# Windowed-attention kernel on one core: each four heads' output products in one visit instead of two, and a new table of slots and banks

## Chip, cores and metric

The kernel runs on one core of a Trainium2 chip. The metric is the device time of one execution in microseconds, as a median of several runs. Engines are named as the profile names them: PE is the matmul engine (TensorE), PEld its weight loads, DVE the vector engine, ACT the scalar engine, POOL GpSimd, SP the engine whose queue issues the DMAs.

## What is computed

Two attention layers follow each other on 64 samples of 14 x 14 tokens with 192 channels. Each layer normalises in 32 groups, projects to 12 heads of 16, adds two relative-position terms to the scores, takes a softmax over 196 keys, multiplies by v, projects back and adds the input.

```python
attn = jnp.einsum('bqd,bkd->bqk', q * scale, k)
rel_h = jnp.einsum('bhwc,hkc->bhwk', qr, Rh)
rel_w = jnp.einsum('bhwc,wkc->bhwk', qr, Rw)
attn = attn.reshape(B * nh, H, W, H, W) + rel_h[:, :, :, :, None] + rel_w[:, :, :, None, :]
attn = jax.nn.softmax(attn.reshape(B * nh, HW, HW), axis=-1)
out = jnp.einsum('bqk,bkd->bqd', attn, v)
...
x = x + _L0_conv_ref(_gn(x), ...)
x = x + _L1_conv_ref(_gn(x), ...)
```

## The kernel before

One unit is one sample in one layer, so there are 128 units. A software pipeline is written out: each turn of the loop on every engine has 12 slots, and work that a table puts at position `at` of a unit is done in slot `at % 12` of turn `at // 12` after that unit's own. In every slot PE makes two pairs of products for two different units: `ps_max` (L510, scores from which DVE takes the row maxima, L704) and `ps_sc` (L523, transposed scores with the maximum folded in, from which ACT makes `probs` by an exponential, L573). `MAX_AT` and `EXP_AT` say where a unit's first head stands. Behind the two pairs of a slot come the jobs of the table `JOBS` that fall on it (each with its position and its bank of `ps_m`), and then the output products.

The jobs, by name: `xT` transposes the input (L420); `g` sums the group statistics (L426); `qk0`, `qk1`, `v` and `y` are projections from high and low fp16 parts (L403); `rel0` to `rel2` are small products for the relative terms on tiles of 64 x 32 of the array (L464); `mT` transposes the maxima (L469); `ot` and `oT` transpose the attention output (L478, L486). `v` and `y` are 12 matmuls each, `qk0` 12, `qk1` 6.

An output product (L542) of one group takes four heads side by side, each on 32 columns of the array, with 98 keys at a time (`kt` 0 and 1); the second half accumulates on the first in the one bank `ps_o`. The program writes four matmuls for a half. The operands are fp32, and the trace shows two records for each, so a half is x8 and both halves are x16. ACT then copies `ps_o` out (L563).

All engines run their own queue in order. PE's next `ps_max` of a bank waits until DVE has reduced the one two heads earlier; `ps_sc` waits likewise for ACT; a job waits until the last reader of its bank is done (`bank_free`); an output product waits until ACT has made the exponentials of its four heads (`s_p`) and has copied `ps_o` (`s_o`). SP issues all DMAs in one order: `q_dram`/`k_dram` out and back in as `q_st`/`k_st`, the relative rows `q_st<-rel_hl`, the maxima row, the result `yo`, the next input `xa`. `ACT_LATER`, `DVE_LATER`, `POOL_AT` and `SP_AT` place each engine's part of a job in its own queue.

Of the kernel before, what the change touches and what calls it, by code (L numbers as in the profile page):

```python
# [15 lines left out]
SIDE = 14  # L16
TOK = SIDE * SIDE
# [5 lines left out]
HEADS = 12  # L23
# [31 lines left out]
HG = 4  # L55
GROUPS = HEADS // HG
# [3 lines left out]
VB = 6  # L60
# [14 lines left out]
def attention_kernel(nc, x_in, w_all, b_qk, b_rows, rel, onehot, lo_rows, ident_in, gmat_in, out):  # L75
    with ExitStack() as ctx:
# [40 lines left out]
        v_st = [sb(f"v_st{i}", [HT, 2, HEADS, PW]) for i in range(VB)]  # L117
# [14 lines left out]
        xn = pair("xn", [CC, 2, TOK])  # L132
# [10 lines left out]
        probs = [sb(f"probs{i}", [HT, 2, TOK]) for i in range(HEADS)]  # L143
        o_sb = pair("o_sb", [128, GROUPS, TOK])
# [10 lines left out]
        ps_o = psum("ps_o", [128, 512])  # L155
# [15 lines left out]
        s_xT = sem("s_xT")  # L171
# [5 lines left out]
        s_g = sem("s_g")  # L177
# [7 lines left out]
        s_qklo = sem("s_qklo")  # L185
        s_v = sem("s_v")
# [7 lines left out]
        s_rlo = sem("s_rlo")  # L194
# [5 lines left out]
        s_mrow = sem("s_mrow")  # L200
# [3 lines left out]
        s_p = sem("s_p")  # L204
        s_o_ps = sem("s_o_ps")
# [40 lines left out]


        LEAD, TAIL = 2, 6
        MAX_AT, EXP_AT = 30, 47

        PV_AT = {(0, 0): 52, (0, 1): 52, (1, 0): 55, (1, 1): 56, (2, 0): 59, (2, 1): 61}
        O_LATER = 1

        JOBS = [(-10, "xT", 1, (s_xT, 1, 1)),
                (63, "ot", 0, (s_on, 1, 1)),
                (4, "qk0", 2, (s_qklo, 2, 1)),
                (5, "qk1", 1, (s_qklo, 2, 2)),
                (65, "oT", 2, (s_olo, 1, 1)),
                (18, "rel0", 0, (s_rlo, 3, 1)),
                (42, "mT", 1, (s_mrow, 1, 1)),  # L260
                (19, "rel1", 2, (s_rlo, 3, 2)),
                (68, "y", 1, (s_yr, 1, 1)),
                (-4, "g", 2, (s_g, 1, 1)),
                (22, "rel2", 2, (s_rlo, 3, 3)),
                (10, "v", 0, (s_v, 1, 1))]
        ORDER = [name for _, name, _, _ in JOBS]
        AT = {name: at for at, name, _, _ in JOBS}
        BANK = {name: bank for _, name, bank, _ in JOBS}
        READ = {name: read for _, name, _, read in JOBS}

        ACT_LATER = {"qk": 0, "mT": 1, "oT": 0, "xT": 0, "rel": 0, "v": 0, "y": 0}
        DVE_LATER = {"bn": 2, "g": 0, "ot": 0, "oT": 0, "qk": 0, "rel": 0}

        POOL_AT = {"mv": -8, "group": -5, "xn": -5, "xhi": -1, "xlo": 3, "y": 72}
        QK_TILES = ((0, 1), (2,))

        SP_AT = {"m": 44, "rel": 23, "qk_out": 6, "q_in": 9, "k_in": 9, "out": 73, "xa": -22}
# [115 lines left out]
        def _(pe):  # L393
# [14 lines left out]
            def job(name, unit, slot, layer):  # L408
# [57 lines left out]
                elif name == "mT":  # L466
                    pe.wait_ge(s_mx, u.n * HEADS + HEADS)
                    bank_free(pe, unit, name)
                    nc.tensor.transpose(ps[0:2 * HEADS, 0:HT], mx[p2][:, :, :].rearrange("p h q -> p (h q)"),  # L469
                                        ident[0:HT, 0:HT]).then_inc(s_mT_ps, 1)  # L470
                elif name == "ot":

                    pe.wait_ge(s_o, u.n * GROUPS + GROUPS)
                    bank_free(pe, unit, name)
                    for h in range(2):
                        for g in range(GROUPS):
                            at = (h * GROUPS + g) * HG * (HD + 1)
# [20 lines left out]

            def iteration(unit, layer):
                for s in range(HEADS):  # L500
# [51 lines left out]
        def _(act):  # L552
            act.wait_ge(s_setup, 1)

            def iteration(unit, layer):
                for s in range(HEADS):

                    for g in range(GROUPS):
                        u = due(unit, s, PV_AT[g, 1] + O_LATER)
                        if u:  # L560
                            act.wait_ge(s_o_ps, u.n * GROUPS + g + 1)
                            wait(act, s_ot_ps, u.n - 1)
                            nc.scalar.copy(o_sb[u.r % 2][:, g, :].rearrange("p (k r b) -> p k r b", r=2, b=SIDE),  # L563
                                           ps_o[:, 0:TOK].rearrange("p (k b r) -> p k r b", r=2, b=SIDE))\
                              .then_inc(s_o, 1)
                    head = head_at(EXP_AT, s)
                    u = due(unit, s, EXP_AT + head)
# [331 lines left out]
```

## Time and profile before

| what | value |
|---|---|
| median of 3 runs | 1927.35 us (1926.01 to 1927.59) |
| the profiled execution | 1927.02 us, span 1925.2 us |
| granted PE clock | 0.996 of full |
| PE busy | 1857.8 us (96%), 34176 matmul records |
| DVE, ACT, POOL busy | 1435.6, 1364.9, 713.3 us |

The first matmul starts at 37.7 us, behind loads and constants. From about 130 us to 1860 us every unit takes the same time. A busy PE is no proof of full use, since a matmul record reaches beyond the moment at which the next one starts. The start of one record to the start of the next is what an instruction costs PE; that is what the prediction reads.

### The profile page before, as it was taken

To read this page: it belongs to the slowest core of one execution; us is meant where nothing else is said; L and a number is where in the kernel's file an instruction comes from. 1 tells how busy PE (TensorE), PEld (TensorE's weight loads), DVE (VectorE), ACT (ScalarE), POOL (GpSimd) and SP (SyncE) were. 2 spreads that over 40 slices of the span, in tenths; PEclk is the share of its full clock that TensorE was granted. 3 is DMA by queue.
4 is the path that set the end of the run, shared out by engine and by line. 5 is a ranking of instruction groups with operands and counts; after the bars stand their busy time and mean duration, and the time that the engine had idled before them with its cause. 6 is when DMAs were issued, how large, how long until landed. Compare 5 with 4: busy or idle time off the path is not lost.

```text
span 1925.2 us, 84394 instructions
## 1 busy us (share of the span) xinstructions
PE 1857.8 (96%) x34176; PEld 1511.5 (79%) x34176; DVE 1435.6 (75%) x3568; ACT 1364.9 (71%) x3201; POOL 713.3 (37%) x1796
## 2 busy tenths in 40 slices
PE   0799999999999999999999999999999999999997
PEld 0678888888888888888888888888888888888885
DVE  6477777777777777777777777777777777777774
ACT  0277777777777777777777777777777777777776
POOL 1333433433434334334334334343343343343331
PEclk9999999999999999999999999999999999999999
DMA  1444444444434444444444444444444444444440
GB/s 39 99 101 102 113 104 108 107 104 108 112 101 113 108 102 110 107 102 112 104 107 108 103 108 112 101 113 105 104 111 107 102 111 105 102 113 104 111 102 25
DMA packets 142171, 197.76 MB, mean 103 GB/s; under 512 B 26455, under 2 KB 109656, under 8 KB 141786
## 3 DMA queue, kind: packets, MB, share of 16 engines
q1 hardware_dynamic: 141786, 192.36, 40.3%
q8 instruction: 274, 4.49, 1.0%
q14 instruction: 111, 0.91, 0.2%
HBM read 97.74 MB, written 57.80 MB: 81 GB/s over the span
## 4 chain that ended last, share of the span: by engine, by line
PE 93%; issue 3%; DVE 2%; POOL 1%; ACT 0%; DMA 0%; POOLq 0%; SPq 0%; ACTq 0%
PE ps_m L403 24%; PE ps_max L510 17%; PE ps_o L542 17%; PE ps_sc L523 13%; PE ps_m L464 11%; PE ps_m L478 4%; PE ps_m L420 2%; PE ps_m L486 2%; PE ps_m L469 1%; PE ps_m L426 1%; DVE k_st L657 0%; POOL yo L840 0%; DVE v_st L650 0%; POOL xn L817 0%; DMA w_raw<-in_b_rows 0%
## 5 line engine op out<-in xcount | busy, mean ns | idle before, releaser
L704 DVE TENSOR_REDUCE mx<-ps_max 98x2 f32<-98x392 f32 x1536 | 834.2, 557 | 237.0 <-PE ps_max L510 222.9
L573 ACT ACTIVATE probs<-ps_sc 98x392 f32<-98x392 f32 x1536 | 735.4, 497 | 171.0 <-PE ps_sc L523 126.0
L510 PE MATMUL ps_max<-k_st,q_st 124*98 124x196 f16 x3072 | 537.8, 257 | 0.6 <-DVE mx L704 0.3
L523 PE MATMUL ps_sc<-q_st,k_st 125*98 125x196 f16 x3072 | 511.3, 247 | 0.6 <-ACT probs L573 0.5
L510 PEld LDWEIGHTS ps_max<-k_st,q_st 124*98 124x98 f16 x3072 | 299.5, 124 | 200.3 <-issue 157.6
L542 PE MATMUL ps_o<-probs,v_st 98*32 98x196 f32 x6144 | 388.7, 340 | 1.9 <-issue 1.1
L523 PEld LDWEIGHTS ps_sc<-q_st,k_st 125*98 125x98 f16 x3072 | 320.5, 124 | 3.5 <-ACT probs L573 1.8
L755 DVE TENSOR_TENSOR rel_hl<-ps_m,rel_hi 128x504 f16<-128x504 f32 (+1 forms) x384 | 216.0, 562 | 85.6 <-ACT rel_hi L618 85.6
L618 ACT ACTIVATE rel_hi<-ps_m,is_lo 128x504 f16<-128x504 f32 (+1 forms) x384 | 225.8, 588 | 31.5 <-PE ps_m L464 31.3
L788 POOL TENSOR_TENSOR msq<-mv 96x2 f32<-96x2 f32 x128 | 24.6, 192 | 586.4 <-DVE mv L730 586.4
L464 PE MATMUL ps_m<-q_st,rel_st 64*32 64x36 f16 (+1 forms) x14336 | 238.0, 209 | 0.3 <-DVE gsm L770 0.3
L464 PEld LDWEIGHTS ps_m<-q_st,rel_st 64*32 64x32 f16 x14336 | 191.5, 101 | 52.3 <-issue 1.3
L798 POOL TENSOR_TENSOR msq<-gsm 96x2 f32<-96x2 f32 x128 | 24.6, 192 | 505.5 <-DVE gsm L770 505.5
L403 PE MATMUL ps_m<-xn_hi,w_hi 98*128 98x196 f16 (+1 forms) x768 | 193.1, 251 | 8.3 <-POOL xn_lo L830 8.3
L542 PEld LDWEIGHTS ps_o<-probs,v_st 98*32 98x32 f32 x6144 | 134.2, 108 | 77.2 <-issue 22.9
L403 PE MATMUL ps_m<-xn_lo,w_hi 96*128 96x196 f16 x768 | 192.1, 250 | 0.0
L403 PE MATMUL ps_m<-xn_hi,w_lo 96*128 96x196 f16 x768 | 191.4, 249 | 0.0
L716 DVE TENSOR_TENSOR qk_hl<-ps_m,qk_hl 128x392 f16<-128x392 f32 (+1 forms) x256 | 117.0, 457 | 79.0 <-ACT qk_hl L585 79.0
L563 ACT COPY o_sb<-ps_o 128x196 f32<-128x196 f32 x384 | 123.9, 323 | 59.0 <-PE ps_o L542 46.7
L585 ACT CAST qk_hl<-ps_m 128x392 f16<-128x392 f32 (+1 forms) x256 | 103.5, 404 | 84.0 <-PE ps_m L403 82.4
L840 POOL TENSOR_TENSOR yo<-yr,xa 98x384 f32<-98x384 f32 x128 | 128.7, 1005 | 55.4 <-ACT yr L632 55.4
L403 PE MATMUL ps_m<-w_hi,xn_hi 98*98 98x192 f16 (+1 forms) x512 | 132.5, 259 | 0.0
(74 smaller groups left out, 2963.8 us busy)
## 6 DMA issues: line engine op xcount, KB each, us to landing
q_st<-q_dram SPq DMA_DIRECT2D x128, 294.0 KB, 3.9
k_st<-k_dram SPq DMA_DIRECT2D x256, 147.0 KB, 3.9
q_dram<-qk_hl SPq DMA_DIRECT2D x128, 147.0 KB, 2.7
k_dram<-qk_hl SPq DMA_DIRECT2D x128, 147.0 KB, 2.8
q_st<-rel_hl SPq DMA_DIRECT2D x256, 73.5 KB
q_st<-rel_hl SPq DMA_DIRECT2D x256, 64.3 KB
xa<-in_x SPq DMA_DIRECT2D x64, 147.0 KB
x<-yo SPq DMA_DIRECT2D x64, 147.0 KB
```

What stands on the lines that cost most here:

```text
L403: last = nc.tensor.matmul(dst, weights(a, c, k), moving(b, c, k), start=n == 0, stop=n == len(terms) - 1)
L464: last = nc.tensor.matmul(to, rel_st[:, lay, axis, w:w + RW], q, start=True, stop=True)
L510: last = nc.tensor.matmul(ps_max[head % 2][0:HT, h * TOK:h * TOK + TOK], q_st[u.n % QB][0:R_MAX, head, h, :], k_st[u.n % QB][0:R_MAX, head ...
L523: last = nc.tensor.matmul(ps_sc[head % 2][0:HT, kt * TOK:kt * TOK + TOK], k_st[u.n % QB][0:STACK, head, kt * HT:kt * HT + HT], q_st[u.n % ...
L542: last = nc.tensor.matmul(ps_o[32 * j:32 * j + 32, 0:TOK], v_st[u.n % VB][:, kt, head_of(head), :], p[:, kt, :], start=kt == 0, stop=kt == 1)
L563: nc.scalar.copy(o_sb[u.r % 2][:, g, :].rearrange("p (k r b) -> p k r b", r=2, b=SIDE), ps_o[:, 0:TOK].rearrange("p (k b r) -> p k r b", r ...
L573: nc.scalar.activation(probs[head][:, :, :], ps_sc[head % 2][0:HT, 0:2 * TOK].rearrange("p (k t) -> p k t", k=2), ACT.Exp, scale=1.0 / (QS ...
L618: nc.scalar.activation(rel_part(rel_hi[u.r % 2], n), rel_bank(n), ACT.Identity, scale=is_lo[:, 0:1]).then_inc(s_rhi, 1)
L704: nc.vector.reduce_max(mx[u.r % 2][:, head, :], ps_max[head % 2][0:HT, 0:2 * TOK].rearrange("p (q k) -> p q k", q=2), axis=AX.X).then_inc( ...
L716: nc.vector.tensor_tensor(qk_hl[u.r % 2][:, 1, at, :], ps_m[BANK[f"qk{j}"]][:, 0:len(tiles) * TOK].rearrange("p (c t) -> p c t", t=TOK), q ...
L755: nc.vector.tensor_tensor(rel_part(rel_hl[u.r % 2], n), rel_bank(n), rel_part(rel_hi[u.r % 2], n), ALU.subtract).then_inc(s_rlo, 1)
L840: nc.gpsimd.tensor_tensor(yo[p2][:, :, :], yr[p2][:, :, :], xa[u.n % XB][:, :, :], ALU.add)\
```

## The change

The two halves of the keys stand in one visit for every group of four heads, and the wait on the four exponentials and on `ps_o` stands ahead of it. The table `PV_AT` has three places in place of six, two of which were one slot before (52). All other tables are new: positions, three banks, and the places in the queues of ACT, DVE, POOL and SP. No instruction of computation is added or removed.

```diff
-        MAX_AT, EXP_AT = 30, 47
-        PV_AT = {(0, 0): 52, (0, 1): 52, (1, 0): 55, (1, 1): 56, (2, 0): 59, (2, 1): 61}
+        MAX_AT, EXP_AT = 29, 45
+        PV = ((0,), (1,), (2,))
+        PV_AT = (50, 53, 56)
         O_LATER = 1
...
-                (-4, "g", 2, (s_g, 1, 1)),
-                (22, "rel2", 2, (s_rlo, 3, 3)),
-                (10, "v", 0, (s_v, 1, 1))]
+                (-5, "g", 0, (s_g, 1, 1)),
+                (20, "rel2", 2, (s_rlo, 3, 3)),
+                (9, "v", 2, (s_v, 1, 1)),
+                (59, "ot", 0, (s_on, 1, 1))]
...
-        SP_AT = {"m": 44, "rel": 23, "qk_out": 6, "q_in": 9, "k_in": 9, "out": 73, "xa": -22}
+        SP_AT = {"m": 41, "rel": 19, "qk_out": 3, "q_in": 9, "k_in": 9, "out": 72, "xa": -21}
...
-                    for (g, kt), at in PV_AT.items():
-                        u = due(unit, s, at)
+                    for i, groups in enumerate(PV):
+                        u = due(unit, s, PV_AT[i])
                         if u:
-                            n = u.n * GROUPS + g
-                            if kt == 0:
+                            if i == 0:
                                 wait(pe, s_v, u.n + 1)
-                                wait(pe, s_p, u.n * HEADS + HG * g + HG)
-                                wait(pe, s_o, n)
-                            for j in range(HG):
-                                head = HG * g + j
-                                p = probs[head]
-                                last = nc.tensor.matmul(ps_o[32 * j:32 * j + 32, 0:TOK],
-                                                        v_st[u.n % VB][:, kt, head_of(head), :], p[:, kt, :],
-                                                        start=kt == 0, stop=kt == 1)
-                            if kt == 1:
+                            wait(pe, s_p, u.n * HEADS + HG * groups[-1] + HG)
+                            wait(pe, s_o, u.n * len(PV) + i)
+                            for n, g in enumerate(groups):
+                                for kt in range(2):
+                                    for j in range(HG):
+                                        head = HG * g + j
+                                        last = nc.tensor.matmul(ps_o[32 * j:32 * j + 32, n * TOK:n * TOK + TOK],
+                                                                v_st[u.n % VB][:, kt, head_of(head), :],
+                                                                probs[head][:, kt, :], start=kt == 0, stop=kt == 1)
                                 last.then_inc(s_o_ps, 1)
```

On PE, this is what stands before around the third group's output products (heads 8 to 11): the first head's scores of the next unit, the first half, two slots without a job, the second half.

```order
L523 MATMUL ps_sc<-q_st,k_st 98x196 [waits s_p,s_m0]
L523 MATMUL ps_sc<-q_st,k_st 98x196
L542 MATMUL ps_o<-probs,v_st 32x196 [waits s_o,s_p,s_v]
L542 MATMUL ps_o<-probs,v_st 32x196 x3
L510 MATMUL ps_max<-k_st,q_st 98x196 [waits s_mx]
L510 MATMUL ps_max<-k_st,q_st 98x196
L523 MATMUL ps_sc<-q_st,k_st 98x196 [waits s_p]
L523 MATMUL ps_sc<-q_st,k_st 98x196
L510 MATMUL ps_max<-k_st,q_st 98x196 [waits s_mx]
L510 MATMUL ps_max<-k_st,q_st 98x196
L523 MATMUL ps_sc<-q_st,k_st 98x196 [waits s_p]
L523 MATMUL ps_sc<-q_st,k_st 98x196
```

The second half (L542 x4) is the next row there. Now, on PE at the same place of the program (line numbers are one higher), the scores ahead are those of head 11 itself, then `rel2`, then both halves:

```order
L524 MATMUL ps_sc<-q_st,k_st 98x196 [waits s_p]
L524 MATMUL ps_sc<-q_st,k_st 98x196
L465 MATMUL ps_m<-q_st,rel_st 32x84 [waits s_rlo]
L465 MATMUL ps_m<-q_st,rel_st 32x84
L465 MATMUL ps_m<-q_st,rel_st 32x6x2 x2
L465 MATMUL ps_m<-q_st,rel_st 32x84 x2
L465 MATMUL ps_m<-q_st,rel_st 32x6x2 x26
L543 MATMUL ps_o<-probs,v_st 32x196 [waits s_o,s_p]
L543 MATMUL ps_o<-probs,v_st 32x196 x7
L511 MATMUL ps_max<-k_st,q_st 98x196 [waits s_mx]
L511 MATMUL ps_max<-k_st,q_st 98x196
```

So the third group's visit moved from one slot after its last head's scores to the same slot, with only `rel2` between, and `rel2` now waits for the low part of `rel1` (`s_rlo`), whose bank it takes, where it waited for `g` before.

In SP's queue, the loads of `q_st` and `k_st` stood ahead of the four DMAs of the relative rows before:

```order
L345 DMA q_st<-mrow 1x24x98 [waits s_mrow]
L365 DMA q_st<-q_dram 64x1x2352 [waits s_qd0]
L371 DMA k_st<-k_dram 32x1x2352 [waits s_kd0]
L371 DMA k_st<-k_dram 32x1x2352
L354 DMA q_st<-rel_hl 32x1176 [waits s_rlo]
L354 DMA q_st<-rel_hl 32x1176
L354 DMA q_st<-rel_hl 28x1176 x2
```

Now they stand behind them:

```order
L346 DMA q_st<-mrow 1x24x98 [waits s_mrow]
L355 DMA q_st<-rel_hl 32x1176 [waits s_rlo]
L355 DMA q_st<-rel_hl 32x1176
L355 DMA q_st<-rel_hl 28x1176 x2
L366 DMA q_st<-q_dram 64x1x2352 [waits s_qd3]
L372 DMA k_st<-k_dram 32x1x2352 [waits s_kd3]
L372 DMA k_st<-k_dram 32x1x2352
```

The load of `q_st` is thus held back until DVE has made the low part of `rel2` of an earlier unit.

## Rows read from the trace of the kernel before

**Rows 1.** Windows: one unit's time; columns are named in the first line.
```profile
core 0: us, PE busy (x) PEld busy (x) DVE busy (x) ACT busy (x) POOL busy (x), PEclk, DMA share, GB/s
1000.00:1014.33 14.33, 14.33 (x270) 11.69 (x269) 10.97 (x28) 10.64 (x26) 5.57 (x16) 1.00 0.43 108
```

**Rows 2.** Timeline of PE, one unit: start, duration, line, tiles, count.
```profile
1002.00 0.25 PE L403 MATMUL ps_m<-xn_hi,w_hi 98*128 98x196 f16 x1
...
1002.93 0.25 PE L403 MATMUL ps_m<-xn_hi,w_lo 96*128 96x196 f16 x1
1003.11 0.87 PE L542 MATMUL ps_o<-probs,v_st 98*32 98x196 f32 x16
1003.91 0.37 PE L510 MATMUL ps_max<-k_st,q_st 124*98 124x196 f16 x2
1004.12 0.33 PE L523 MATMUL ps_sc<-q_st,k_st 125*98 125x196 f16 x2
...
1006.70 0.66 PE L464 MATMUL ps_m<-q_st,rel_st 64*32 64x84 f16 x40
1007.29 0.54 PE L542 MATMUL ps_o<-probs,v_st 98*32 98x196 f32 x8
1007.76 0.37 PE L510 MATMUL ps_max<-k_st,q_st 124*98 124x196 f16 x2
1007.96 0.33 PE L523 MATMUL ps_sc<-q_st,k_st 125*98 125x196 f16 x2
1008.14 0.25 PE L403 MATMUL ps_m<-w_hi,oT_hi 98*98 98x192 f16 x1
...
1009.13 0.26 PE L426 MATMUL ps_m<-mv,gmat 96*96 96x4 f32 x2
1009.32 0.54 PE L542 MATMUL ps_o<-probs,v_st 98*32 98x196 f32 x8
1009.79 0.37 PE L510 MATMUL ps_max<-k_st,q_st 124*98 124x196 f16 x2
1010.00 0.33 PE L523 MATMUL ps_sc<-q_st,k_st 125*98 125x196 f16 x2
...
1010.60 0.52 PE L464 MATMUL ps_m<-q_st,rel_st 64*32 64x84 f16 x32
1011.05 0.28 PE L403 MATMUL ps_m<-w_hi,xn_hi 98*98 98x192 f16 x1
...
1012.08 0.33 PE L510 MATMUL ps_max<-k_st,q_st 124*98 124x196 f16 x2
1012.25 0.33 PE L523 MATMUL ps_sc<-q_st,k_st 125*98 125x196 f16 x2
1012.52 0.54 PE L542 MATMUL ps_o<-probs,v_st 98*32 98x196 f32 x8
1012.99 0.37 PE L510 MATMUL ps_max<-k_st,q_st 124*98 124x196 f16 x2
...
1016.32 0.25 PE L403 MATMUL ps_m<-xn_hi,w_hi 98*128 98x196 f16 x1
```

**Rows 3.** Timeline of ACT and PE: two steady exponentials, and the last output products.
```profile
1010.37 0.89 ACT L573 ACTIVATE probs<-ps_sc 98x392 f32<-98x392 f32 x2
...
1912.68 0.89 ACT L573 ACTIVATE probs<-ps_sc 98x392 f32<-98x392 f32 x2
...
1913.66 0.87 PE L542 MATMUL ps_o<-probs,v_st 98*32 98x196 f32 x16 [0.85 <-ACT probs L573]
```

**Rows 4.** Timeline of DVE and POOL: from the group sums to the normalised input.
```profile
1009.43 0.16 DVE L770 COPY gsm<-ps_m 96x4 f32<-96x4 f32 x1
...
1012.88 0.51 POOL L825 CAST xn_hi<-xn 96x392 f16<-96x392 f32 x1
...
1014.31 0.93 POOL L830 TENSOR_TENSOR xn_lo<-xn,xn_hi 96x392 f16<-96x392 f32 x1
```

**Rows 5.** SP's issues in order of time, then q_st's load's time to landing.
```profile
1011.97 2.88 SPq L354 DMA_DIRECT2D q_st<-rel_hl  x4
...
DMA to landing us min/median/max: 3.5/3.9/4.5
```

More of the change, by code:

```diff
@@ L248, in attention_kernel @@
         LEAD, TAIL = 2, 6
-        MAX_AT, EXP_AT = 30, 47
-        PV_AT = {(0, 0): 52, (0, 1): 52, (1, 0): 55, (1, 1): 56, (2, 0): 59, (2, 1): 61}
+        MAX_AT, EXP_AT = 29, 45
+        PV = ((0,), (1,), (2,))
+        PV_AT = (50, 53, 56)
         O_LATER = 1
[L254 to L262, printed above, removed]
-                (-4, "g", 2, (s_g, 1, 1)),
-                (22, "rel2", 2, (s_rlo, 3, 3)),
-                (10, "v", 0, (s_v, 1, 1))]
+        JOBS = [(-11, "xT", 1, (s_xT, 1, 1)),
+                (2, "qk0", 2, (s_qklo, 2, 1)),
+                (4, "qk1", 1, (s_qklo, 2, 2)),
+                (64, "oT", 2, (s_olo, 1, 1)),
+                (17, "rel0", 0, (s_rlo, 3, 1)),
+                (41, "mT", 1, (s_mrow, 1, 1)),
+                (18, "rel1", 2, (s_rlo, 3, 2)),
+                (67, "y", 1, (s_yr, 1, 1)),
+                (-5, "g", 0, (s_g, 1, 1)),
+                (20, "rel2", 2, (s_rlo, 3, 3)),
+                (9, "v", 2, (s_v, 1, 1)),
+                (59, "ot", 0, (s_on, 1, 1))]
         ORDER = [name for _, name, _, _ in JOBS]
@@ L269, in attention_kernel @@
         READ = {name: read for _, name, _, read in JOBS}
-        ACT_LATER = {"qk": 0, "mT": 1, "oT": 0, "xT": 0, "rel": 0, "v": 0, "y": 0}
-        DVE_LATER = {"bn": 2, "g": 0, "ot": 0, "oT": 0, "qk": 0, "rel": 0}
-        POOL_AT = {"mv": -8, "group": -5, "xn": -5, "xhi": -1, "xlo": 3, "y": 72}
+        ACT_LATER = {"qk": 0, "mT": 0, "oT": 0, "xT": 0, "rel": 0, "v": 0, "y": 1}
+        DVE_LATER = {"bn": 0, "g": 0, "ot": 1, "oT": 0, "qk": 0, "rel": 0}
+        POOL_AT = {"mv": -7, "group": -5, "xn": -3, "xhi": 0, "xlo": 0, "y": 77}
         QK_TILES = ((0, 1), (2,))
-        SP_AT = {"m": 44, "rel": 23, "qk_out": 6, "q_in": 9, "k_in": 9, "out": 73, "xa": -22}
+        SP_AT = {"m": 41, "rel": 19, "qk_out": 3, "q_in": 9, "k_in": 9, "out": 72, "xa": -21}
         def head_at(base, slot):
@@ L471, in job @@
                 elif name == "ot":
-                    pe.wait_ge(s_o, u.n * GROUPS + GROUPS)
+                    pe.wait_ge(s_o, u.n * len(PV) + len(PV))
                     bank_free(pe, unit, name)
@@ L556, in iteration @@
                 for s in range(HEADS):
-                    for g in range(GROUPS):
-                        u = due(unit, s, PV_AT[g, 1] + O_LATER)
+                    for i, groups in enumerate(PV):
+                        u = due(unit, s, PV_AT[i] + O_LATER)
                         if u:
-                            act.wait_ge(s_o_ps, u.n * GROUPS + g + 1)
+                            act.wait_ge(s_o_ps, u.n * GROUPS + groups[-1] + 1)
                             wait(act, s_ot_ps, u.n - 1)
-                            nc.scalar.copy(o_sb[u.r % 2][:, g, :].rearrange("p (k r b) -> p k r b", r=2, b=SIDE),
-                                           ps_o[:, 0:TOK].rearrange("p (k b r) -> p k r b", r=2, b=SIDE))\
+                            nc.scalar.copy(o_sb[u.r % 2][:, groups[0]:groups[-1] + 1, :]
+                                           .rearrange("p g (k r b) -> p (g k) r b", r=2, b=SIDE),
+                                           ps_o[:, 0:len(groups) * TOK].rearrange("p (k b r) -> p k r b", r=2, b=SIDE))\
                               .then_inc(s_o, 1)
```

## Prediction

> **What bounds the kernel now.** I read the table of windows first: in a stretch as long as one unit PE is busy for all of its 14.33 us, while DVE works 10.97 us and ACT 10.64 us [rows 1]. A full PE bar proves little, so I then read PE's timeline by starts. The reader is to see that each start follows the last at the same small distance: the two pairs of a slot are 0.17 us apart, 0.085 us a matmul (12.08 to 12.25), and nowhere in the unit does a matmul wait for another engine. The first matmul of `qk0` at 1002.00 comes again at 1016.32, 14.33 us later by the windows' length [rows 1, 2]. So PE's own instructions, with what it loses when it changes from one kind of tile to another, are the time: 128 x 14.33 = 1834 us of the 1925 us span, and the rest is the start and the drain. What PE saves per unit counts in full, until some wait becomes visible.
>
> **What the change removes.** It removes no matmul, only boundaries. Their price, by starts [rows 2]:
> - Into an output visit from full-width work: the pair of scores at 12.25 is followed at 12.52, 0.27 us and not 0.17; for `qk0`, 2.93 to 3.11 is 0.18 and not 0.085. So 0.09 us more (I take 0.09).
> - The visit itself up to the next `ps_max`: 0.47 us for one half (12.52 to 12.99, also at 7.29 and 9.32), and 0.80 us for both (3.11 to 3.91). Two halves apart are 0.94, together 0.80.
> - Out of it: the pair behind it takes 0.21 or 0.20 us (3.91 to 4.12, 7.76 to 7.96) and not 0.17, so 0.04 more.
>
> One half on its own therefore costs 0.09 + 0.47 + 0.04 = 0.60 us, both together 0.93 us. The four lone halves now:
> - third group, two visits behind scores: 0.60 + 0.60;
> - second group, first half, behind `rel1`: no entry to take off, since `rel1` is itself tiled, 0.47 + 0.04 = 0.51;
> - second group, second half, behind `g`: 0.51. The way from `g` to it is 0.19 us (9.13 to 9.32), and the way from `g` to an ordinary pair is in no row. It can be no less than two steps of 0.03 to 0.085 and no more than the 0.19. I take 0.13, near the middle, so 0.06 us goes here, with 0 and 0.10 as ends.
>
> Sum removed: 0.60 + 0.60 + 0.51 + 0.51 + 0.06 = 2.28 us a unit.
>
> **What it adds.** The second group's visit now follows `mT`, a full-width job: 0.93 us. The third follows `rel2`; `rel2` to the next thing is 0.45 us (10.60 to 11.05), and I take that exit as it is, so 0.84 us. `rel1` is now followed by an ordinary pair, which takes 0.04 more, as a pair behind a visit does; bounds are 0 and 0.09 (an entry's price). `v` no longer follows `rel2`: it took 1.03 us (11.05 to 12.08) where `y`, the same 12 matmuls, takes 0.99 (8.14 to 9.13), so 0.04 less. Sum added: 0.93 + 0.84 + 0.04 - 0.04 = 1.77 us. PE's own work per unit goes down by 2.28 - 1.77 = **0.51 us**, to 13.82 us, if nothing waits. That is 65 us over 128 units.
>
> The Trainium skill (TensorEngine Tiling (Array Packing), Tiling Modes, Key Properties) says that a change of tiling mode drains the array. By that rule every visit pays one way in and one way out whatever stands beside it, so two visits less would bring 2 x (0.60 + 0.60 - 0.93) = 0.54 us, 69 us in all. The trace agrees for full-width neighbours, but from `rel1` into a visit [rows 2] no extra shows beyond what `rel2` pays to any successor, and I keep the 0.51 of the rows.
>
> **The wait that it adds.** The third group's visit needs the exponential of head 11, and that head's scores are now made in the same slot. Count from the slot's start. The scores start at 0.17; ACT starts their exponential 0.37 us after them (10.00 to 10.37), at 0.54, if it is free, and it is, since the slot before gave it only one more exponential after `rel1`. It runs 0.50 us (two in 0.89, the second starting 0.39 after the first), until 1.04 [rows 2, 3]. PE takes up an output visit 0.10 us after that: at the end of the run two exponentials end at 1912.68 + 0.89 = 1913.57 and the visit that waited for them starts at 1913.66 or 1913.67 [rows 3]. So it can start at 1.14. PE itself arrives at 0.17 + 0.26 (scores and entry into `rel2`, as into a visit) + 0.45 = 0.88. It **waits 0.26 us**; after an idle gap the first of the four passes is a little shorter, and I take 0.24 us (bounds 0.20 and 0.28). Behind the waiting matmul stand all later pairs, so DVE and ACT get theirs later too. No job is there to cover it. Before, the same exponential had most of a slot more. Over about 125 units in which the slot is full: 30 us.
>
> **Other waits that come nearer.** I walked the slots in the new order with these prices. Slots 5, 6 and 7 last 2.0, 1.1 and 1.5 us, slot 8 lasts 1.7, slot 2 lasts 2.3.
> - `qk0` needs the low part of the normalised input. From `gsm` (9.43) to the end of `xn_hi` (13.39) are 3.96 us, and `xn_lo`, now directly behind it, takes 0.07 to begin and 0.93: 4.96 us [rows 4]. `gsm` starts 0.30 us after `g` (9.13 to 9.43), and now up to 0.70, since a maximum is in front. With 0.05 to react, `qk0` can start 5.3 to 5.7 us after `g`. PE's way from `g` to `qk0` was 7.19 us (9.13 to 16.32); less 2.28 - 0.51 for visits gone in that stretch, less one slot's two pairs 0.34, plus the third visit's 0.80, it is 5.88, and 6.12 with the wait. Just hidden, by 0.2 to 0.8 us.
> - The load of `q_st` now waits in SP's queue for `rel2`. From the start of slot 8: `rel2` ends at 0.9, ACT and DVE make its two parts by about 1.9, the four DMAs take SP 2.88, the load lands 3.9 later (at most 4.5): 8.7 to 9.3 us [rows 5]. `rel0` needs it at 13.82 - (2.0 + 1.1 + 1.5) + 0.43 = 9.65, 9.9 with the wait. Hidden by 0.6 to 1.2 us.
> - DVE's share rises to 10.97 of about 14.06 us, which leaves room; its queue is longest in slots 0 to 2 (division, statistics, two maxima), where my walk finds its maximum due within 0.1 us of PE's need.
>
> **Sum.** 1927.0 (the profiled execution, 0.3 below the median) - 65 + 30 = **1892 us**. The unit's time should be 13.82 + 0.24 = 14.06 us. The ends of the unknown prices are 0.05 us a unit for the exits, 0.04 for the wait, and some 3 us for start and drain, whose latency chains move: 1884 to 1900 for this case.
>
> **Rivals.**
> 1. *No wait shows* (the exponential comes earlier than I count, or `rel2` takes longer). Then 1927 - 65 = 1862 us. Against it stand three durations of rows that leave 0.26 us. Chance 8%.
> 2. *More than one wait shows*: one of the three slim covers fails by 0.1 to 0.25 us a unit, 12 to 31 us more, 1904 to 1923. For it: the covers are estimates of 0.1 to 0.6 us. Chance 14%.
> 3. *No change that can be told* (within 0.2%, 3.9 us): the waits together eat the 0.51. The covers would have to fail by 0.27 us beyond the wait. Chance 3%.
> 4. *Slower, by the load of `q_st`*. It is behind the relative rows and behind their wait for DVE. If it lands more than 0.6 to 1.2 us later than now, PE waits at `rel0` every unit; 0.27 us beyond that the kernel is as slow as before, and at 1 us more beyond, it takes 1927 + 0.73 x 125 = 2018 us or less, as the chain slackens. For it: all relative rows are in front of it in the queue. Against: the four DMAs need 2.88 us only to be issued, so most of their bytes have gone, and landing times spread only from 3.5 to 4.5 [rows 5]. Chance 4%.
>
> **How the numbers follow.** The forecast has 71%. Faster by over 0.2% holds in it and in rivals 1 and 2: 93%. The range reaches from 1880, somewhat below the forecast's own 1884, up to 1910 into rival 2; below lies rival 1 (8%), above the rest of rival 2 and rivals 3 and 4 (some 12%).
>
> **What would show it.** In the new profile the output visits are x16 alone, three a unit, each 0.80 us to the next `ps_max`; the unit repeats every 14.06 us; PE has one wait a unit, on the exponential of ACT ahead of the visit behind `rel2`, with starts 0.7 and not 0.45 us after `rel2` begins. If the gap there is missing, rival 1 is at work. If gaps stand ahead of `qk0`, `rel0` or a `ps_max`, it is rival 2 or 4. I would be wrong above all if a wait that I count as hidden by 0.2 us is not.

## The result and the profile after

| kernel | median | of |
|---|---|---|
| before | 1927.30 us (1926.01 to 1927.59) | 4 runs |
| after | 1894.20 us (1894.12 to 1894.75) | 4 runs |

The ratio is 0.983, with a 95% interval of 0.9813 to 0.9847: 33 us less. The forecast was 1892 us.

The head of the page of the changed kernel:

```profile
span 1892.3 us, 84394 instructions
...
PE 1807.1 (95%) x34176; PEld 1533.1 (81%) x34176; DVE 1401.2 (74%) x3568; ACT 1352.2 (71%) x3201; POOL 712.6 (38%) x1796
```

The window of one unit, with the columns of [rows 1]:

```profile
1000.00:1014.05 14.05, 13.91 (x271) 11.74 (x266) 10.57 (x28) 10.50 (x25) 5.57 (x14) 1.00 0.45 106
```

The number of PE records is the same, 34176, and PE's bar is still nearly full. Unlike before it has a gap in a unit, though: 13.91 us busy of 14.05. PE's timeline, which answers to [rows 2], tells where:

```profile
1003.26 0.26 PE L470 MATMUL ps_m<-ident,mx 98*24 98x98 f32 x1
1003.45 0.87 PE L543 MATMUL ps_o<-probs,v_st 98*32 98x196 f32 x16
1004.25 0.37 PE L511 MATMUL ps_max<-k_st,q_st 124*98 124x196 f16 x2
...
1004.72 0.67 PE L465 MATMUL ps_m<-q_st,rel_st 64*32 64x84 f16 x40
1005.31 0.37 PE L511 MATMUL ps_max<-k_st,q_st 124*98 124x196 f16 x2
...
1006.69 0.26 PE L427 MATMUL ps_m<-mv,gmat 96*96 96x4 f32 x2
1006.80 0.35 PE L511 MATMUL ps_max<-k_st,q_st 124*98 124x196 f16 x2
1006.99 0.33 PE L524 MATMUL ps_sc<-q_st,k_st 125*98 125x196 f16 x2
1007.25 0.52 PE L465 MATMUL ps_m<-q_st,rel_st 64*32 64x84 f16 x32
1007.91 0.87 PE L543 MATMUL ps_o<-probs,v_st 98*32 98x196 f32 x16
1008.72 0.37 PE L511 MATMUL ps_max<-k_st,q_st 124*98 124x196 f16 x2
1009.00 0.37 PE L524 MATMUL ps_sc<-q_st,k_st 125*98 125x196 f16 x2
```

Every visit is x16 and is followed 0.80 or 0.81 us later by the next `ps_max` (1003.45 to 1004.25, 1007.91 to 1008.72). From `rel2` to the visit behind it are 0.66 us (1007.25 to 1007.91), where `rel2` to its successor took 0.45 us in [rows 2]. The records overlap, so of these 0.21 us more PE's row shows only 0.14 us as idle (14.05 - 13.91); the distance of starts gives the whole. The weight loader's line in the list of waits names its cause (engine line waited for: us in total, times, longest):

```profile
PEld ps_o L543 <- ACT probs L574: 32.0, 128, 0.8
...
PE ps_sc L524 <- DMA q_st<-mrow: 2.7, 6, 0.9
```

The first is the forecast wait, 128 times, 0.25 us each: idle time of the weight loader, of which 0.21 us reach the matmuls. The second was not forecast. It shows in the timeline too: behind the pair at 1008.72 the next one starts 0.28 us later, not 0.21. ACT's timeline shows the releaser of the first:

```profile
1007.36 0.50 ACT L574 ACTIVATE probs<-ps_sc 98x392 f32<-98x392 f32 x1 [0.78 <-PE ps_sc L524]
```

The scores of head 11 start at 1006.99, their exponential at 1007.36, and it ends at 1007.86. The visit starts at 1007.91.

From here on "the unit" is the mean over 105 units in the middle of the run, worked out from the starts of `xT` of unit 15 and unit 120: 14.339 us before ((1745.99 - 240.43) / 14.339 = 105) and 14.084 us after ((1716.22 - 237.38) / 105). A unit in which nothing is late takes 14.05 us. 128 x (14.339 - 14.084) = 33 us, the whole difference of the medians. In the experiments this product and the difference of the medians agree within 5 us, but for one run (7 us), whose unit holds stretches at a lower clock, as said there.

### The profile page after: what moved, and what is told of

Same layout as the page of the kernel before. It is cut to its first block, busy times and chain, and to the rows that moved or that the text cites. A ratio compares the mean times of both kernels' runs of the same rounds, so it can differ in the third digit from the quotient of the medians.

```text
span 1892.3 us, 84394 instructions
## 1 busy us (share of the span) xinstructions
PE 1807.1 (95%) x34176; PEld 1533.1 (81%) x34176; DVE 1401.2 (74%) x3568; ACT 1352.2 (71%) x3201; POOL 712.6 (38%) x1796
## 4 chain that ended last, share of the span: by engine, by line
PE 86%; issue 4%; ACT 4%; DVE 2%; DMA 2%; SPq 1%; POOL 1%; POOLq 0%; ACTq 0%
PE ps_m L404 23%; PE ps_max L511 17%; PE ps_o L543 16%; PE ps_sc L524 13%; PE ps_m L465 8%; PE ps_m L479 4%; ACT probs L574 3%; PE ps_m L421 2%; PE ps_m L487 2%; DMA q_st<-mrow 1%; PE ps_m L470 1%; SPq L337 1%; PE ps_m L427 1%; DVE k_st L658 0%; POOL yo L841 0%
## 5 line engine op out<-in xcount | busy, mean ns | idle before, releaser
L574 ACT ACTIVATE probs<-ps_sc 98x392 f32<-98x392 f32 x1536 | 722.9, 497 | 201.8 <-PE ps_sc L524 157.7
L511 PEld LDWEIGHTS ps_max<-k_st,q_st 124*98 124x98 f16 x3072 | 292.1, 124 | 133.0 <-issue 80.3
L543 PE MATMUL ps_o<-probs,v_st 98*32 98x196 f32 x6144 | 335.7, 336 | 18.8 <-ACT probs L574 1.8
L543 PEld LDWEIGHTS ps_o<-probs,v_st 98*32 98x32 f32 x6144 | 159.9, 109 | 93.6 <-ACT probs L574 32.0
L404 PE MATMUL ps_m<-w_hi,xn_hi 98*98 98x192 f16 (+1 forms) x512 | 127.7, 249 | 1.8 <-DVE rel_hl L756 1.7
```

The lines of the kernel that those rows point to most:

```text
L404: last = nc.tensor.matmul(dst, weights(a, c, k), moving(b, c, k), start=n == 0, stop=n == len(terms) - 1)
L511: last = nc.tensor.matmul(ps_max[head % 2][0:HT, h * TOK:h * TOK + TOK], q_st[u.n % QB][0:R_MAX, head, h, :], k_st[u.n % QB][0:R_MAX, head ...
L543: last = nc.tensor.matmul(ps_o[32 * j:32 * j + 32, n * TOK:n * TOK + TOK], v_st[u.n % VB][:, kt, head_of(head), :], probs[head][:, kt, :], ...
L574: nc.scalar.activation(probs[head][:, :, :], ps_sc[head % 2][0:HT, 0:2 * TOK].rearrange("p (k t) -> p k t", k=2), ACT.Exp, scale=1.0 / (QS ...
```

## Experiments

Ratios are to the kernel before on the same chip (1926.97 to 1927.29 us there), with the 95% interval. "Old table" is the kernel before with the named edit, "new table" the changed one.

### What one visit in place of two is worth

**Old table, third group at 60, second at 55.** It changes three numbers of the kernel before and leaves its banks and queues alone.
```diff
-        PV_AT = {(0, 0): 52, (0, 1): 52, (1, 0): 55, (1, 1): 56, (2, 0): 59, (2, 1): 61}
+        PV_AT = {(0, 0): 52, (0, 1): 52, (1, 0): 55, (1, 1): 55, (2, 0): 60, (2, 1): 60}
```


> The old table again, all three groups merged, but groups 1 and 2 put at positions 55 and 60: behind rel1, so that g stays late enough, and in slot 0, between the empty slots, so that no maximum pair comes under 1.0 us after the one two slots earlier. Boundaries: 0.51 + 0.06 + 0.60 - 2 x 0.33 = 0.50 us a unit less, a unit of 13.84 us. Theory: no wait appears, 1864 us, which is 30 us faster than the changed kernel with only three numbers of the old table touched. Rival: a new table was needed for the merge, and waits for ACT, DVE or POOL (qk0's cover by POOL is down to about 0.1 us) eat 0.25 us and more: 1895 us or above.

Measured: 1866.85 us, ratio 0.9687 (0.9673 to 0.9701), unit 13.847 us. Its window of one unit:
```profile
1000.00:1013.84 13.84, 13.84 (x269) 11.82 (x268) 10.87 (x28) 10.55 (x26) 5.57 (x14) 1.00 0.42 111
```
And one line of PE's timeline that comes again 13.84 us later:
```profile
1011.90 0.50 PE L420 MATMUL ps_m<-ident,xa 98*96 98x98 f32 x4
...
1025.74 0.50 PE L420 MATMUL ps_m<-ident,xa 98*96 98x98 f32 x4
```
PE waits for nothing in the unit, and the boundaries alone took 14.339 - 13.847 = 0.49 us off it. The new table is not needed for the gain. It is 27 us slower than this edit.

**New table with the first two groups split again** (halves at 50 and 51, 53 and 54, the third group whole at 56):
```diff
-        PV_AT = (50, 53, 56)
+        PV_AT = (51, 54, 56)
+        HALF_AT = {(0, 0): 50, (0, 1): 51, (1, 0): 53, (1, 1): 54, (2, 0): 56, (2, 1): 56}
...
```
The loop of the output products goes over `HALF_AT` here, one half at a time, with the waits ahead of the first half.

> The changed kernel's table, but groups 0 and 1 are split again into two visits (positions 50 and 51, 53 and 54); group 2 stays merged behind rel2. If the gain comes from the merge, at my prices group 0 costs 0.27 us more and group 1 0.47 + 0.04 - 0.04 - 0.33 = 0.14 us more a unit, together 0.40: 1941 us, slower than before. Rival: the gain of the change comes from its new positions and banks, and the split costs little: 1894 to 1905 us.

Measured: 1944.33 us, 1.0089 (1.0074 to 1.0104), unit 14.476. Splitting the two groups costs 14.476 - 14.084 = 0.39 us a unit, where 0.40 was expected. This kernel has four lone halves, as many as the kernel before, and with its new wait it takes 0.14 us a unit more than that. So the gain of the change is the merging, and none of it the layout.

**Old table, 56 and 61**: the merged visits stand where the second halves stood.
```diff
-        PV_AT = {(0, 0): 52, (0, 1): 52, (1, 0): 55, (1, 1): 56, (2, 0): 59, (2, 1): 61}
+        PV_AT = {(0, 0): 52, (0, 1): 52, (1, 0): 56, (1, 1): 56, (2, 0): 61, (2, 1): 61}
```


> The old table with one thing changed: the first halves of groups 1 and 2 are moved to where their second halves stood (positions 56 and 61), so that all three visits hold both halves. By boundaries alone PE saves 0.51 + 0.60 - 2 x 0.33 - 0.04 = 0.40 us a unit, and the time would be 1876 us (rival: only PE's own instructions count, any merge pays). My theory says that two waits appear: g comes 0.47 us earlier and waits about 0.3 us for DVE's low part of rel1, whose bank it takes; and slots 11, 0 and 1 stand three in a row with nothing but their two pairs (0.34 us each), where the maximum pair of a slot must come at least about 1.0 us after the one two slots earlier (0.37 to the reduction, 0.56 for it, 0.05 to react), so that slot 1 waits about 0.34 us for DVE. Then the unit takes about 14.5 us and the time is 1940 to 1960 us, slower than before.

Measured: 1973.27 us, 1.0241 (1.0224 to 1.0258), unit 14.710. The sign was as expected, the size was not. PE's timeline:
```profile
1003.33 0.25 PE L403 MATMUL ps_m<-w_hi,oT_lo 96*98 96x192 f16 x1
1003.75 0.30 PE L426 MATMUL ps_m<-mv,gmat 96*96 96x4 f32 x2 [0.18 <-DVE rel_hl L755]
...
1007.43 0.33 PE L510 MATMUL ps_max<-k_st,q_st 124*98 124x196 f16 x2
1007.60 0.33 PE L523 MATMUL ps_sc<-q_st,k_st 125*98 125x196 f16 x2
1008.07 0.37 PE L510 MATMUL ps_max<-k_st,q_st 124*98 124x196 f16 x2
```
Two waits stand there, each in nearly every unit. `g` starts 0.42 us behind the last matmul of `y` in place of 0.08, since DVE hasn't finished `rel1`'s low part, which `g` waits for to have its bank: the half visit behind `rel1` had covered that. And the maximum pair at 1008.07 starts 0.47 us behind the pair at 1007.60 in place of 0.17. The two waits, 0.34 and 0.31 us, leave 14.339 + 0.65 - 14.710 = 0.28 us for what the boundaries saved, where 0.40 was expected: that is most of why it is slower than the 1940 to 1960 us.

**Old table, third group at 59** with the second at 55:
```diff
-        PV_AT = {(0, 0): 52, (0, 1): 52, (1, 0): 55, (1, 1): 56, (2, 0): 59, (2, 1): 61}
+        PV_AT = {(0, 0): 52, (0, 1): 52, (1, 0): 55, (1, 1): 55, (2, 0): 59, (2, 1): 59}
```


> The merged old table once more (55 and 60 gave a unit of 13.85 us without a wait), but group 2 at 59, in slot 11, so that slots 0 and 1 hold only their two pairs (0.38 and 0.34 us) and slot 2 starts 0.72 us after slot 0. Boundaries are the same. Theory: a maximum pair must come about 1.04 us after the one two slots earlier (0.41 to the reduction behind a visit, 0.56, 0.05, and a start of the weights 0.04 late costs nothing), so slot 2 waits 0.3 us for DVE: 14.16 us a unit, 1905 us. Rival: the place of the visit among short slots does not matter, 1867 us.

Measured: 1907.87 us, 0.9899 (0.9883 to 0.9916), unit 14.186, as expected. It isolates the second of those waits. PE's timeline:
```profile
1003.72 0.37 PE L510 MATMUL ps_max<-k_st,q_st 124*98 124x196 f16 x2
...
1004.10 0.33 PE L510 MATMUL ps_max<-k_st,q_st 124*98 124x196 f16 x2
1004.27 0.33 PE L523 MATMUL ps_sc<-q_st,k_st 125*98 125x196 f16 x2
1004.75 0.37 PE L510 MATMUL ps_max<-k_st,q_st 124*98 124x196 f16 x2
```
and DVE's:
```profile
1004.13 2.27 DVE L704 TENSOR_REDUCE mx<-ps_max 98x2 f32<-98x392 f32 x4 [0.71 <-PE ps_max L510]
```
The maxima alternate between two banks. DVE starts on the pair of 1003.72 at 1004.13 and needs 2.27 / 4 = 0.57 us, so the same bank is free at 1004.70, and PE refills it at 1004.75, 1.03 us after it was filled last. Without the wait it would come after 0.38 + 0.34 = 0.72 us. A slot with nothing in it but its two pairs therefore can't stand beside another such slot without a wait of 0.3 us. The half visit at 59 or 61 was the filling.

### The new wait behind rel2

**New table, third group one slot later.**
```diff
-        PV_AT = (50, 53, 56)
+        PV_AT = (50, 53, 57)
```


> The changed kernel with the visit of group 2 one slot later (57, behind v). In the changed kernel 0.306 us lie between the last product of rel2 and that visit, against 0.098 from rel2 to v before. Theory: 0.208 us of it is the wait for the exponential of head 11, and it goes; the entry from full-width work (0.09) and the pair behind rel2 (0.04) come in its place, so PE saves 0.08 us a unit. But the scores of head 0 of the next unit, which stand in slot 9, now come 1.0 us earlier, and the DMA of the maxima row lands only about 1.0 us ahead of them at the median: a new wait of about 0.25 us on average, 1905 to 1925 us. Rival: the 0.306 us are the cost of changing from one tiling to another, no wait: then the gap stays in some form, and nothing else waits, 1894 us or more by 5.

Measured: 1979.64 us, 1.0272 (1.0255 to 1.0289), unit 14.807. The wait on the exponential is gone, but PE waits elsewhere, and longer:
```profile
1007.75 0.52 PE L465 MATMUL ps_m<-q_st,rel_st 64*32 64x84 f16 x32
1008.20 0.37 PE L511 MATMUL ps_max<-k_st,q_st 124*98 124x196 f16 x2
1008.49 0.37 PE L524 MATMUL ps_sc<-q_st,k_st 125*98 125x196 f16 x2
1009.24 0.26 PE L404 MATMUL ps_m<-w_hi,xn_hi 98*98 98x192 f16 x1 [0.39 <-DVE rel_hl L756]
```
and in its list of waits:
```profile
PE ps_sc L524 <- DMA q_st<-mrow: 27.4, 37, 1.8
```
`rel2` to its successor is 0.45 us again, so what stood behind it in the changed kernel was a wait of 0.66 - 0.45 = 0.21 us. But `v` is given `rel2`'s bank, and now has only one slot's pairs between them: it starts 0.75 us after the scores, not 0.17 (0.83 us in most units, where the scores themselves are in time). The visit had covered the two readers of that bank, ACT and DVE. The expectation had left this out, and so was wrong by more than 50 us. (New banks in the change have `g` and `v` only, two jobs and not three.) The maxima row, too, is late in 37 units and not in 6.

The execution that was profiled took 1990.67 us, 11 us more than the median, and its clock tells why. Where the wait for the maxima row was long, PE's granted clock could fall behind it from full to half, 2.4 to 1.2 GHz, for 6.8 us (a row of PE, then the window behind it with the columns of [rows 1]):
```profile
1141.98 0.37 PE L524 MATMUL ps_sc<-q_st,k_st 125*98 125x196 f16 x2 [1.30 <-DMA q_st<-mrow]
```
```profile
1142.60:1149.40 6.80, 6.80 (x49) 5.65 (x47) 1.97 (x5) 2.58 (x6) 2.12 (x5) 0.50 0.51 126
```
There are five such stretches between 200 us and the drain, each begun in or within 0.6 us behind a wait of PE on this DMA of 1.1 to 1.8 us; three waits of 1.2 to 1.4 us were followed by none. A unit with one takes 3.9 to 4.4 us more, the wait included. The unit of 14.807 us is a mean with three of them in it. The median unit is 14.65 us, as in the next run.

**The same, with the next input's load behind the maxima row in SP's queue.**
```diff
-        PV_AT = (50, 53, 56)
+        PV_AT = (50, 53, 57)
...
-        SP_AT = {"m": 41, "rel": 19, "qk_out": 3, "q_in": 9, "k_in": 9, "out": 72, "xa": -21}
+        SP_AT = {"m": 41, "rel": 19, "qk_out": 3, "q_in": 9, "k_in": 9, "out": 72, "xa": -19}
```


> As the run with the visit of group 2 at 57, and SP issues xa behind the maxima row (-19 for -21), which gives that DMA about 0.5 us back. Theory: most of the new wait goes, 0.05 us a unit stays, about 1888 us. If the two runs are equal, the wait at head 0's scores is not that DMA.

Measured: 1962.27 us, 1.0183 (1.0168 to 1.0198), unit 14.653. The 17 us between the medians of the two runs went with the maxima row's DMA: its waits, and the stretches at half clock behind them. How they divide is not shown; the mean clock was 0.990 to 0.994 in the four other executions there and 0.995 to 0.997 here. The rest of the loss is `v`'s bank. 1888 us was expected, so this was a miss of the same cause.

**The same again, with `v` and `rel2` in different banks.**
```diff
-        JOBS = [(-11, "xT", 1, (s_xT, 1, 1)),
+        JOBS = [(-11, "xT", 0, (s_xT, 1, 1)),
...
-                (9, "v", 2, (s_v, 1, 1)),
+                (9, "v", 0, (s_v, 1, 1)),
...
-                (59, "ot", 0, (s_on, 1, 1))]
+                (59, "ot", 1, (s_on, 1, 1))]
```


> The changed kernel with group 2 at 57 and xa at -19 as in the earlier run, and v in bank 0, ot in bank 1, xT in bank 0. In the earlier run v, which takes rel2's bank, waited 0.66 us for DVE's low part of rel2, because the visit that had covered it was gone from between. Theory: with another bank for v that wait goes, no wait for an exponential is left, and the unit takes 14.05 - 0.21 + 0.09 + 0.04 = 13.97 us, with 0.02 for late DMAs of the maxima row 13.99: 1881 us. Rival: the head-0 scores then find that DMA late in most units, as I had expected of the first of these runs: 1895 us or more.

Measured: 1879.46 us, 0.9754 (0.974 to 0.9769), unit 13.990. The place behind `rel2` was good for the boundary and bad for the exponential: leaving it saves 0.21 us and costs an entry and a pair's 0.04, 0.13 us by [rows 2], so that 0.08 us should remain. The unit fell by 0.06 us against the kernel with the same SP queue and the visit at 56 (14.054, below).

**A longer `rel2`**: `RELB`, the blocks of relative products of the three jobs, from (6, 6, 2) to (6, 2, 6), so that `rel2` covers the exponential, with `v` and `ot` in other banks and four DMAs of SP's queue at other places.
```diff
-RELB = (6, 6, 2)
+RELB = (6, 2, 6)
...
-                (9, "v", 2, (s_v, 1, 1)),
+                (9, "v", 0, (s_v, 1, 1)),
...
-                (59, "ot", 0, (s_on, 1, 1))]
+                (59, "ot", 2, (s_on, 1, 1))]
...
-        SP_AT = {"m": 41, "rel": 19, "qk_out": 3, "q_in": 9, "k_in": 9, "out": 72, "xa": -21}
+        SP_AT = {"m": 41, "rel": 20, "qk_out": 3, "q_in": 7, "k_in": 7, "out": 72, "xa": -19}
```


> The changed kernel with the relative rows cut 6, 2, 6 and not 6, 6, 2: the short piece stands in slot 6 and a long one (0.60 and not 0.45 us) between head 11's scores and the visit of group 2. PE's own work is the same. So that nothing else waits, v takes bank 0 and ot bank 2, SP issues the loads of q_st and k_st at position 7, the relative rows at 20 behind them, and xa at -19. Theory: the wait for head 11's exponential goes from 0.21 to 0.06 us a unit and the waits for the maxima row go: 14.09 - 0.15 - 0.03 = 13.91 us a unit, 1872 us. Rival (the gap ahead of the visit is the price of a change of tiling, not a wait): 1890 us.

Measured: 1941.92 us, 1.0074 (1.0059 to 1.0089), unit 14.493. A miss, again by a bank:
```profile
1006.18 0.33 PE L524 MATMUL ps_sc<-q_st,k_st 125*98 125x196 f16 x2
1006.94 0.24 PE L404 MATMUL ps_m<-xn_hi,w_hi 98*128 98x196 f16 x1 [0.42 <-DVE on L742]
```
`qk0` starts 0.76 us after the scores, not 0.17: it has the bank that `ot` got, and DVE reads `ot` for the division until then.

**The same with `ot` in bank 1 and `xT` in bank 0.**
```diff
-        JOBS = [(-11, "xT", 1, (s_xT, 1, 1)),
+        JOBS = [(-11, "xT", 0, (s_xT, 1, 1)),
...
-                (59, "ot", 2, (s_on, 1, 1))]
+                (59, "ot", 1, (s_on, 1, 1))]
```


> The long-rel2 kernel again (rows cut 6, 2, 6, v in bank 0, loads of q_st at 7, relative rows at 20, xa at -19), with ot in bank 1 and xT in bank 0, so that qk0 no longer takes the bank that DVE's division of ot still reads. In its predecessor the gap ahead of the visit behind rel2 fell to 0.191 us (rel1, as long, pays 0.128 to any successor), and qk0 waited 0.58 us for that bank. Theory: with the bank changed the 0.58 us go and nothing comes: a unit of 14.49 - 0.58 = 13.91 us, 1871 us. Rival: qk0 was late for another reason (the low part of the normalised input from POOL, whose cover I put at 0.1 to 0.3 us): then part of the wait stays, 1885 us or more.

Measured: 1870.3 us, 0.9703 (0.9689 to 0.9718), unit 13.910, as expected. PE:
```profile
1007.66 0.66 PE L465 MATMUL ps_m<-q_st,rel_st 64*32 64x84 f16 x40
1008.32 0.87 PE L543 MATMUL ps_o<-probs,v_st 98*32 98x196 f32 x16
```
The visit now follows a `rel2` of x40 by 0.66 us, where `rel1` of the same size is followed by 0.59. Most of the wait is filled with work that has to be done anyway: 14.054 - 13.910 = 0.14 us a unit.

### The maxima row's DMA

**Changed kernel, the input's load behind the maxima row and not ahead of it in SP's queue.**
```diff
-        SP_AT = {"m": 41, "rel": 19, "qk_out": 3, "q_in": 9, "k_in": 9, "out": 72, "xa": -21}
+        SP_AT = {"m": 41, "rel": 19, "qk_out": 3, "q_in": 9, "k_in": 9, "out": 72, "xa": -19}
```


> The changed kernel with one number changed: SP issues the next input (xa) at position -19 and not -21, so that the small DMA of the maxima row is issued ahead of it, about 0.5 us earlier. In the changed kernel's trace the scores of head 0 wait in 11 of 112 units for that DMA, up to 0.6 us, 0.03 us a unit on average. Theory: these waits go, 1890 us, and every unit takes 14.05 us. Rival: these waits come from something else that is there in some units (a busy DMA engine of the q_st load): no change, 1894 us.

Measured: 1890.24 us, 0.9809 (0.9795 to 0.9824), unit 14.054. In the list of waits PE and its weight loader have no line on `mrow` any more. (The 11 units of the expectation count the same units twice: in the middle of the run 6 weight loads and 5 matmuls waited.) 14.084 - 14.054 = 0.03 us a unit is what the late rows cost, 4 us in all. The interval overlaps that of the change (0.9813 to 0.9847), so that the 4 us rest on the unit and on the waits gone, not on the medians alone.

### How far it goes

**Old table, the first group directly behind `rel0` at 54** (from 52), `mT` one slot later, and ACT's part of `mT` in its own slot:
```diff
-        PV_AT = {(0, 0): 52, (0, 1): 52, (1, 0): 55, (1, 1): 56, (2, 0): 59, (2, 1): 61}
+        PV_AT = {(0, 0): 54, (0, 1): 54, (1, 0): 55, (1, 1): 55, (2, 0): 60, (2, 1): 60}
...
-                (42, "mT", 1, (s_mrow, 1, 1)),
+                (43, "mT", 1, (s_mrow, 1, 1)),
...
-        ACT_LATER = {"qk": 0, "mT": 1, "oT": 0, "xT": 0, "rel": 0, "v": 0, "y": 0}
+        ACT_LATER = {"qk": 0, "mT": 0, "oT": 0, "xT": 0, "rel": 0, "v": 0, "y": 0}
```


> The merged old table (55 and 60), and group 0 moved from 52, behind qk0, to 54, directly behind rel0, with mT one position later (43, and ACT's part of it without delay), so that it stands ahead of rel1. By boundaries: qk0 gives up its exit into a visit (0.18 to 0.08), rel0's exit of 0.13 goes into the visit and not into mT, mT's exit goes into rel1 (0.19 and not 0.09 plus 0.18 of the scores before it): 0.09 us a unit less, a unit of 13.76 us, 1855 us, if no wait comes. Rival: what a visit costs does not depend on what stands ahead of it (a drain is paid for every change of tiling, rel1 into a visit too): 1867 us. A wait by g for rel1's low part or by the visit for exponentials would show as a gap and make it slower than 1867.

Measured: 1928.28 us, 1.0007 (0.9997 to 1.0017), unit 14.339. PE's timeline:
```profile
1001.75 0.25 PE L403 MATMUL ps_m<-xn_hi,w_lo 96*128 96x196 f16 x1
1002.42 0.51 PE L486 MATMUL ps_m<-ident,on 98*96 98x98 f32 x4 [0.42 <-DVE qk_hl L716]
```
and its list of waits:
```profile
PE ps_m L486 <- DVE qk_hl L716: 51.2, 123, 0.4
```
1855 us was expected, so this was a miss. The boundary was saved as priced, and all of it and more was lost at one place: `oT`, which takes `qk0`'s bank, starts 0.67 us after the last matmul of `qk1` and not 0.08, since DVE still reads `qk0`. The visit at 52 had stood between them.

**The same, with one tile in `qk0` and two in `qk1`**:
```diff
-        QK_TILES = ((0, 1), (2,))
+        QK_TILES = ((0,), (1, 2))
```


> The last kernel (visits at 54, 55 and 60) with qk0 taking one tile (6 matmuls) and qk1 two (12), where it was two and one. In the last run every boundary came out as priced, 13.76 us a unit without waits, but oT, which takes qk0's bank, waited 0.58 us for DVE's low part of qk0: the visit of group 0 had stood between them and covered it. Now 12 matmuls of qk1 stand between, 0.51 us more, and qk0's read is shorter by a tile. Theory: the 0.58 us go, nothing else waits, 13.76 us a unit and 1855 us, the fastest. Rival: the saving behind tiled work is paid again elsewhere, because DVE and POOL are near their limit of slots (qk1 now ends later than mT or rel1 need): 1867 us or more.

Measured: 1853.27 us, 0.9619 (0.9602 to 0.9636), unit 13.747: the fastest kernel of this study, 3.8% faster than before and 2.2% faster than the change. Its window of one unit:
```profile
1000.00:1013.75 13.75, 13.75 (x274) 11.85 (x267) 10.77 (x27) 10.63 (x25) 5.56 (x15) 1.00 0.44 112
```
And in PE's timeline the two visits that stand behind tiled work:
```profile
1005.16 0.67 PE L464 MATMUL ps_m<-q_st,rel_st 64*32 64x84 f16 x40
1005.76 0.87 PE L542 MATMUL ps_o<-probs,v_st 98*32 98x196 f32 x16
...
1007.12 0.67 PE L464 MATMUL ps_m<-q_st,rel_st 64*32 64x84 f16 x40
1007.71 0.87 PE L542 MATMUL ps_o<-probs,v_st 98*32 98x196 f32 x16
```
`qk0` is now half as much to read, and 12 matmuls stand between it and `oT` in place of 6, which covers the reading again. From `rel` to the visit are 0.60 and 0.59 us, the same as from `rel` to an ordinary pair (0.59). The entry into the visit costs nothing there.

## Why the prediction held

**PE was the bound, and what its instructions save counts in full.** Right. The two kernels without a recurring wait have the unit that prices by starts gave ahead of the runs, 13.84 and 13.76 us: it is 13.847 us, and 13.747 with one entry into a visit less (0.09 of the 0.10). And 128 times the difference of the units is the difference of the medians for the change, and is within 3 us of it for these two.

**The removed and added boundaries, 0.51 us.** Right within 0.02. The old table with its visits merged saved 0.49 us without a wait. In the changed kernel, 14.084 less the two waits, 0.21 and 0.03, is 13.85 us, 0.49 below before. Both halves cost 0.80 us to the next pair, as in [rows 2]. The price that no row had, from `g` to a pair, was taken as 0.13 us; it is 0.11 (1006.69 to 1006.80), and the pair behind it takes 0.19 in place of 0.17, which makes up the 0.13. The Trainium skill's rule (TensorEngine Tiling (Array Packing), Tiling Modes, Key Properties), by which each change of mode drains the array, gave 0.54 us. Here the trace agrees for full-width neighbours, where a visit pays 0.09 us going in and 0.04 behind it. Behind `rel` it does not: the kernels with a visit there show nothing beyond `rel`'s own exit, and so the lone half behind `rel1` in the kernel before had no entry to give back.

**The new wait.** The right place, the right releaser, in every unit. Its size was 0.21 us and not 0.24 (0.26 by the durations). The term that was mis-sized is the time to react, taken as 0.10 us from the end of the run [rows 3]. Here the exponential ends at 1007.86 and the visit starts at 1007.91, 0.05 us. With 0.05 in place of 0.10 the durations give 0.21. The further 0.02 us that the prediction took off, for a shorter first pass after an idle gap, was not there: the visit takes 0.81 us to the next pair, as elsewhere. That makes 0.03 us a unit against the forecast 0.24, some 4 us in all. That the gap was a wait and no price of the boundary was shown by taking the visit away from `rel2` (0.45 us again) and by filling the gap (0.14 us off the unit).

**The covers.** Those named held. `xn_lo` ended at 1012.25 by POOL's row below, and `qk0` started at 1012.91, 0.66 us later; no recurring wait of `rel0` on the load of `q_st` is listed, though it landed 3.9 us after issue as before. The maximum of slot 2, called within 0.1 us of PE's need, just met it: the reduction it waits for, the second row, ended at 1012.48, and the pair started at 1012.56, 0.34 us behind `xT` as in the kernel before.
```profile
1011.32 0.93 POOL L831 TENSOR_TENSOR xn_lo<-xn,xn_hi 96x392 f16<-96x392 f32 x1
...
1011.91 0.57 DVE L705 TENSOR_REDUCE mx<-ps_max 98x2 f32<-98x392 f32 x1 [0.30 <-PE ps_max L511]
```
One cover was not named: the maxima row's DMA of 4.6 KB, which the new table puts behind another load on SP, nearer to its first reader (issued 4.2 us ahead of it, and 4.7 us before). It is late in a few units only, so that no median of a boundary shows it, and costs 0.03 us a unit (4 us). The two errors, 4 us each, went opposite ways; the 0.02 us of the boundaries are another 3 us, against a miss of 2 us in all. That the forecast came so close is thus luck in part: each of the three was worth more than the miss, and one of them was a wait that the prediction had not seen.

**Rival 2**, a slim cover that fails, was the one to take more seriously as a mechanism, though not here: in four of the experiments an unforeseen wait was what decided, each time at a bank of `ps_m` that was still being read. In two more, waits at banks of `ps_m` and `ps_max` decided that had been foreseen.

## What to carry to other kernels

Price a piece of work on a tiled array by the distances of starts, entry, body and exit apart, and put tiled work behind other tiled work: here two halves apart, behind full-width work, cost 1.20 us with their boundaries, together 0.93, and together behind `rel` 0.84. Before moving such a piece, list what it covered, above all who still reads the bank that the job behind it will overwrite, the exponential it needs, and small DMAs with little slack. A cover that was forgotten cost 0.6 to 0.7 us a unit here, more than the 0.49 us of the whole merging, and a bank number or one tile moved from a job to the next gave it back.

## What was unexpected of the hardware

- The step from an engine's end to the start of the matmul that waits for it is not one number. It is 0.05 us behind ACT's exponential (1007.86 to 1007.91, and the same in all 128 units for the weight load) and behind DVE's reduction (1004.70 to 1004.75). It is 0.15 us behind the TENSOR_TENSOR rows of DVE that `g`, `v`, `qk0` and `oT` waited for in five of the experiments; with the first group at 54 the row below ends at 1002.27 and `oT` starts at 1002.42. At the drain of the run it is 0.10 us behind an exponential [rows 3]. In the cases of 0.15 and 0.10 us, 0.03 stand between the start of the weight load and that of its matmul, in the others none. Why the rest differs stays open.
```profile
1001.70 0.57 DVE L716 TENSOR_TENSOR qk_hl<-ps_m,qk_hl 128x392 f16<-128x392 f32 x1 [0.44 <-ACT qk_hl L585]
```
- Matmuls of a visit behind `rel` start with no delay beyond `rel`'s own exit, although the tile changes from 64 x 32 to 98 x 32: 0.59 to 0.60 us from `rel` of x40 to either kind of successor.
- The maxima row's DMA, the same in every unit, kept PE waiting in 6 of 128 units in the changed kernel, by up to 0.9 us near the start and 0.4 us later, and in 37 by up to 1.8 us with the third group one slot later. A median over units hides that. Behind five of the long waits the granted clock was half for 6.8 us, which cost more than the wait itself: two runs with the same median unit of 14.65 us had medians 17 us apart.
